# A feed-forward layer taken tile by tile instead of in pairs, with its keys as rows, and a second buffer of probabilities

## What is computed

```python
x = x + xattn(layernorm(x), ctx)     # 8 heads of 128; ctx has 2 x 77 = 154 rows of 384
x = x + ffn(layernorm(x))

# xattn: sim = q k^T * 128**-0.5, (sim - mean) * 1.5 + mean, softmax over 154 keys, times v, heads joined, Wout, + bout
# ffn, over the rows t of a batch:
x_prev = concat([zeros, x[:, :-1, :]])
xr = mu_r * x + (1 - mu_r) * x_prev
xk = mu_k * x + (1 - mu_k) * x_prev
out = sigmoid(xr @ W_r) * (square(relu(xk @ W_k)) @ W_v)
```

## Time and profile before

| | before |
|---|---|
| three timed runs, median (lowest to highest) | 744.74 us (743.87 to 744.83) |
| the profiled execution, its own time | 744.54 us |
| its span, first to last instruction | 742.7 us |
| TensorE busy | 736.4 us, 99% of the span |
| VectorE, ScalarE, GpSimd busy | 516.0, 426.8, 123.7 us |
| moved by DMA | 106.52 MB, mean 143 GB/s |

### The profile page before, as it was taken

One profiled execution on the slowest core, in us unless ns is written; L12 is line 12 of the kernel. 1 busy time (PEld: TensorE's weight loads), 2 busy tenths in 40 slices (PEclk: granted clock), 3 DMA queues, 4 the chain that ended last, 5 costly groups with the idle time before them and its releaser, 6 DMA issues.

```text
span 742.7 us, 13556 instructions
## 1 busy us (share of the span) xinstructions
PE 736.4 (99%) x3948; PEld 643.0 (87%) x3948; DVE 516.0 (69%) x1085; ACT 426.8 (57%) x1204; POOL 123.7 (17%) x279
## 2 busy tenths in 40 slices
PE   9999999999999999999999999999999999999998
PEld 8957888888988888898888889888888988888887
DVE  3678987777667766666776766677666667766662
ACT  3568865575746556564655656465665646565332
POOL 1111111202121120212112021211202121120211
PEclk9999999999999999999999999999999999999999
...
GB/s 330 252 152 172 202 136 115 148 147 177 140 146 147 117 164 87 176 142 167 129 109 159 93 175 144 163 126 115 167 84 175 143 167 128 109 156 93 112 28 43
DMA packets 87239, 106.52 MB, mean 143 GB/s; under 512 B 9999, under 2 KB 64169, under 8 KB 87211
## 3 DMA queue, kind: packets, MB, share of 16 engines
...
HBM read 58.70 MB, written 47.45 MB: 143 GB/s over the span
## 4 chain that ended last, share of the span: by engine, by line
PE 90%; SPq 5%; DVE 1%; DMA 1%; ACT 1%; issue 1%; POOL 0%; POOLq 0%; DVEq 0%
PE ffn L494 12%; PE ffn L496 12%; PE ffn L495 12%; PE scores L495 9%; PE scores L496 9%; PE scores L494 9%; PE attended L496 9%; PE attended L495 9%; PE attended L494 9%; SPq L353 3%; SPq L336 1%; PE attended L544 1%; PE attended L543 1%; DMA x_rows<-normed 1%; SPq L333 1%
## 5 line engine op out<-in xcount | busy, mean ns | idle before, releaser
L494 PE MATMUL scores<-A_hi,xT_hi 128*128 128x462 f32 x372 | 129.9, 349 | 0.8 <-DVE B_lo L973 0.8
L495 PE MATMUL scores<-A_lo,xT_hi 128*128 128x462 f32 x372 | 130.4, 351 | 0.0
L496 PE MATMUL scores<-A_hi,xT_lo 128*128 128x462 f32 x372 | 130.0, 349 | 0.0
L775 ACT ACTIVATE probs<-scores,neg_max 128x154 f32<-128x154 f32 x248 | 93.2, 387 | 46.7 <-DVE neg_max L1033 46.6
L496 PE MATMUL attended<-B_hi,pT_lo 128*128 128x512 f32 x288 | 112.5, 391 | 0.0
L495 PE MATMUL attended<-B_lo,pT_hi 128*128 128x512 f32 x288 | 112.4, 390 | 0.0
L494 PE MATMUL attended<-B_hi,pT_hi 128*128 128x512 f32 x288 | 112.1, 389 | 0.0
L1033 DVE TENSOR_REDUCE neg_max<-scores 128x3 f32<-128x462 f32 (+1 forms) x93 | 53.3, 581 | 80.9 <-PE scores L496 80.9
L1334 POOL TENSOR_SCALAR var<-stats 128x1 f32<-128x1 f32 x64 | 13.2, 206 | 462.4 <-DVE stats L979 461.3
L494 PEld LDWEIGHTS scores<-A_hi,xT_hi 128*128 128x128 f32 x372 | 70.2, 189 | 8.0 <-issue 1.7
L495 PEld LDWEIGHTS scores<-A_lo,xT_hi 128*128 128x128 f32 x372 | 70.1, 188 | 5.6
...
## 6 DMA issues: line engine op xcount, KB each, us to landing
...
probs_handed<-prob_rows SPq DMA_DIRECT2D x128, 176.0 KB, 3.4
...
```

Source lines behind the costliest of these rows:

```text
L494: te.matmul(psum, left[0], right[0], start=first, stop=False)
L495: te.matmul(psum, left[0], right[1], start=False, stop=False)
L496: return te.matmul(psum, left[1], right[0], start=False, stop=last)
L775: last = nc.scalar.activation(probs[:, q, cols], score_banks(t)[b][:, (h - h0) * J:(h - h0 + 1) * J], ACT.Exp, bias=neg_max[:, h:h + 1], a ...
```

## The change

The feed-forward part goes tile by tile, one step behind attention. In step t TensorE makes scores(t + 2), attend(t), `key_rows`(t - 1), `gate_rows`(t - 1) and `value_rows`(t - 2). `key_rows` takes the tile as stationary operand and the weights as moving one: 12 matmuls of 512 columns. Its result has rows on the partitions, so the squares now take the road through DRAM as well: `store_squares`, `hand_squares` (five DMAs more for a tile on SyncE's queue), `squares_turn` on VectorE; for the last tile TensorE turns them (`turn_last_squares`, 4 transposes). `handed2` and `act_handed` are landing buffers of their own, there are two buffers `probs`, the halo is kept for every tile and not for every pair, `add_x` stands ahead of `x_turn`, probabilities are handed back one step later, and in the ramp the first exponentials of tile 1 stand ahead of the first `values_hi`. W_v's raw rows land elsewhere, after a wait for `wq_turned`. The ramp on each engine and the last steps are rewritten for the new order. The core of the diff:

```diff
         handed = sb("handed", [P, D])
+        handed2 = sb("handed2", [P, D])
...
-        probs = sb("probs", [P, 4, WIDE])
-        probs_high = probs[:].bitcast(F32R)
+        probs = [sb(f"probs{i}", [P, 4, WIDE]) for i in range(2)]
+        probs_high = [p[:].bitcast(F32R) for p in probs]
...
-            mixed[w] = sb(f"x{w}", [P, DC, 2 * P])
-            mixed_lo[w] = sb(f"x{w}_lo", [P, DC, 2 * P], F32R, at=at_mixed)
-            mixed_hi[w] = sb(f"x{w}_hi", [P, DC, 2 * P], F32R)
-        at_act = cursor[0]
-        act = sb("act", [P, DC, 2 * P])
-        act_lo = sb("act_lo", [P, DC, 2 * P], F32R, at=at_act)
-        act_hi = sb("act_hi", [P, DC, 2 * P], F32R)
+            mixed[w] = sb(f"x{w}", [P, DC, P])
+            mixed_lo[w] = sb(f"x{w}_lo", [P, DC, P], F32R, at=at_mixed)
+            mixed_hi[w] = sb(f"x{w}_hi", [P, DC, P], F32R)
+        act = sb("act", [P, D])
+        act_handed = sb("act_handed", [P, D])
+        at_actT = cursor[0]
+        actT = sb("actT", [P, DC, P])
+        act_lo = sb("act_lo", [P, DC, P], F32R, at=at_actT)
+        act_hi = sb("act_hi", [P, DC, P], F32R)
         at_gate = cursor[0]
...
+            def store_squares(t):
+                sp.wait_ge(square_ready, t + 1)
+                sp.dma_start(act_dram[bass.ds(t * P, P), :], act[:]).then_inc(act_stored, 16)
+
+            def hand_squares(t):
+                sp.wait_ge(act_stored, 16 * (t + 1))
+                if begun(t - 1):
+                    sp.wait_ge(act_turned, t)
+                hand(act_handed, act_dram, t, act_landed)
...
+            def key_rows(t):
+
+                if begun(t - 1):
+                    te.wait_ge(relu_ready, t)
+                else:
+                    te.wait_ge(W_ready, DC)
+                te.wait_ge(mixed_split["k"], t + 1)
+                ffn_rows(T[1], (mixed_hi["k"], mixed_lo["k"]), WT["k"]).then_inc(k_done, 1)
+
...
-            def key_columns(q):
-
-                te.wait_ge(mixed_split["k"], 2 * q + 2)
-                for j in range(2):
-                    if begun(q - 1):
-                        te.wait_ge(gated, 2 * q + j - 1)
-                    for m in (2 * j, 2 * j + 1):
-                        for c in range(DC):
-                            cols = tuple(w[:, c, m * P:(m + 1) * P] for w in WT["k"])
-                            last = three_passes(T[1 + j][:, (m % 2) * 2 * P:(m % 2 + 1) * 2 * P], cols,
-                                                (mixed_hi["k"][:, c, :], mixed_lo["k"][:, c, :]),
-                                                c == 0, c == DC - 1)
-                    last.then_inc(k_done, 1)
-
...
+            def turn_last_squares():
+
+                te.wait_ge(square_ready, TILES)
+                for c in range(DC):
+                    last = te.transpose(S[1][:, c * P:(c + 1) * P], normed[:, c * P:(c + 1) * P], identity[:])
+                last.then_inc(act_turned, 1)
+
...
             def step(g, s):
-                t, q, half = place(g, s)
+                t = place(g, s)
                 if is_tile(t + 2):
                     scores(t + 2)
                 if is_tile(t):
                     attend(t)
-                if is_pair(q) and half == 0:
-                    gate_rows(q, 0)
-                    key_columns(q)
-                if is_pair(q) and half == 1:
-                    gate_rows(q, 1)
-                    value_rows(q, 0)
-                    if is_last(t):
-                        turn_last_x2()
-                    if is_pair(q + 1):
-                        value_rows(q, 1)
-                    else:
-                        last_value_rows()
+                if is_last(t):
+                    value_rows(t - 3)
+                key_rows(t - 1)
+                gate_rows(t - 1, turn_last_x2 if is_last(t) else None)
+                if is_last(t - 1):
+                    turn_last_squares()
+                if not is_last(t + 1):
+                    value_rows(t - 2)
+                if is_last(t - 1):
+                    last_value_rows()
...
+            scores(4)
+            attend(2)
+            key_rows(0)
+            gate_rows(0)
+            scores(5)
+            key_rows(1)
+            gate_rows(1)
+            attend(3)
+            value_rows(0)
+            key_rows(2)
+            gate_rows(2)
+            value_rows(1)
             turns(te, step)
...
+            def squares(t):
+                act_e.wait_ge(k_done, t + 1)
+                if is_last(t):
+                    act_e.wait_ge(xn_stored, 16 * (TILES - 2))
+                if begun(t - 1):
+                    act_e.wait_ge(act_stored, 16 * t)
+                nc.scalar.activation(act[:], T[1][:], ACT.Relu).then_inc(relu_ready, 1)
+                act_e.wait_ge(relu_ready, t + 1)
+                to, rows = (in_quarters(normed), by_quarter(act)) if is_last(t) else (act[:], act[:])
+                nc.scalar.activation(to, rows, ACT.Square).then_inc(square_ready, 1)
+
...
             def step(g, s):
-                t, q, half = place(g, s)
-                if is_pair(q) and half == 1:
-                    squares(q, 1)
-                    squares_hi(q)
+                t = place(g, s)
                 if comes_in_steps(t + 3):
                     x_norm(t + 3, (s + 3) % 4)
                 if is_tile(t + 2):
-                    for b in range(3):
-                        exponentials(t + 2, b)
-                    normalise_early(t + 2)
-                if is_tile(t - 1):
-                    mixed_high("k", t - 1, 1 - half)
-                    mixed_high("r", t - 1, 1 - half)
+                    exponentials(t + 2, s % 2, 0)
+                mixed_high("k", t - 1)
+                if is_tile(t + 2):
+                    exponentials(t + 2, s % 2, 1)
+                if not is_last(t) and not is_last(t - 1):
+                    squares_hi(t - 2)
+                mixed_high("r", t - 1)
+                if is_tile(t + 2):
+                    exponentials(t + 2, s % 2, 2)
+                    normalise_early(t + 2, s % 2)
+                    pack_hi(t + 2, s % 2)
                 if is_tile(t + 3):
                     x_hi(t + 3)
-                if is_tile(t + 2):
-                    pack_hi(t + 2)
-                if is_pair(q):
-                    open_gate(q, half, t)
                 if is_tile(t):
                     x2_norm(t, s)
+                if is_last(t) or is_last(t - 1):
+                    squares_hi(t - 2)
+                squares(t - 1)
                 if is_tile(t + 1):
                     for i in range(3):
                         probs_hi(t + 1, i)
-                if is_pair(q) and half == 0:
-                    squares(q, 0)
+                open_gate(t - 1, (s + 1) % 2)
+                if is_last(t - 1):
+                    squares_hi(t - 1)
 
             nc.scalar.dma_start(ctx1[:], ctx_rows[P:J, :]).then_inc(ctx_loaded, 16)
...
+                exponentials(0, 0, b)
+            normalise_early(0, 0)
+            pack_hi(0, 0)
             x_norm(3, 3)
-            for b in range(2):
-                values_hi(2 * b)
-                values_hi(2 * b + 1)
-                exponentials(1, b)
+            exponentials(1, 1, 0)
+            for b in range(1, 3):
...
-            normalise_early(4)
+                exponentials(4, 0, b)
+            normalise_early(4, 0)
             x_hi(5)
-            mixed_high("r", 1, 1)
-            open_gate(0, 0, 2)
-            pack_hi(4)
+            pack_hi(4, 0)
+            squares(0)
             x2_norm(2, 2)
+            mixed_high("k", 1)
             for i in range(3):
                 probs_hi(3, i)
-            squares(0, 0)
-            turns(act_e, step, from_second=True)
+            open_gate(0, 0)
+            x_norm(6, 2)
+            mixed_high("r", 1)
+            for b in range(2):
+                exponentials(5, 1, b)
+            squares_hi(0)
+            exponentials(5, 1, 2)
+            normalise_early(5, 1)
+            squares(1)
+            mixed_high("k", 2)
+            pack_hi(5, 1)
+            x_hi(6)
+            open_gate(1, 1)
+            mixed_high("r", 2)
+            squares_hi(1)
...
             for w in "kr":
-                mix(w, 0, 0, 0)
+                mix(w, 0)
             for b in range(3):
                 maxima(4, b)
             for w in "kr":
-                mixed_low(w, 0, 0)
-            x2_turn(1, 1, 0)
-            mix_change(1, 1, 0)
-            mix("k", 1, 1, 0)
+                mixed_low(w, 0)
             inverse_early(4)
-            mixed_low("k", 1, 1)
+            x_turn(5)
+            normalise_late(4, 0)
+            x_lo(5)
+            x2_turn(1)
+            pack_lo(4, 0)
+            mix_change(1)
             add_x(2, 0, 2)
-            normalise_late(4)
-            x_turn(5)
-            mix("r", 1, 1, 0)
-            x_lo(5)
-            mixed_low("r", 1, 1)
-            pack_lo(4)
             probs_turn(3)
+            mix("k", 1)
```

(48 more changed lines are left out.)

448 lines of the change are left out of this document (232 added, 216 removed).

## The result

The changed kernel took **742.38 us** (median of 9 executions, 741.68 to 743.74), the kernel before, run beside it, 744.18 (743.03 to 745.71): ratio 0.9976, 95% interval 0.9967 to 0.9984, so 1.8 us less (below, the interval stands in brackets behind each ratio). Run once more later, it gave 742.25 and 0.9975 [0.9963, 0.9987]. The forecast of 744.8 was 2.4 too high; it said "no change" and there is a small gain.

The account below looks back on a forecast made before the run. TensorE, busy 99% of the span, was taken as the bound. -5.1 - 0.1 + 1.5 + 1.1 + 2.0 + 0.8 + 0.4 - 0.5 = +0.1 us on 744.74 gave 744.8; range 741.2 to 747.8 for 8 in 10.

Parts of the forecast that it names:

- 1.1 us ahead of value_rows(1): Ramp: TensorE waits 1.1 us for open_values(0) before tile 1's value rows; bounds 0 and 2.5.
- 0.8 us ahead of turn_last_squares: Last steps: TensorE waits 0.8 us for squares(31), behind tile 30's squares through DRAM; bounds 0 and 2.
- the start, -0.1: Start: only 0.1 us saved, as tile 0's probabilities come back at 60.6 us regardless; bounds 0 and 1.9.
- Wait 1.5 us in front of gate_rows(1): Ramp: TensorE waits 1.5 us, xr's high part standing behind x_norm(6) on ScalarE; bounds 0.5 and 2.5.
- Keys, -5.1: TensorE's key rows: 384 matmuls of 512 columns replace 768 of 256, saving 5.1 us; bounds 4.6 to 5.6.
- The loop adds nothing: Tiles 4 to 28: no added wait, step 21.47 us; least reserve 2 us at the squares, 4 more behind.
- Rival B: Loop: the squares' way through DRAM holds each step, landing 6 us later than walked; slower, 749.8 us; 12%.
- Wait 2.0 us ahead of attend(31): Last steps: TensorE waits 2.0 us for probs_hi(31), squares(29) standing in front on ScalarE; bounds 1.0 and 2.5.
- Old wait -0.5: Last steps: the earlier 0.5 us wait ahead of the turn of the last tile's second x goes.
- transposes +0.4: TensorE's four new transposes for the last tile's squares add 0.4 us.
- Rival A: Other engines run ahead of the walk, three of four waits vanish; faster, 739.4 to 742.5 us; 22%.
- four gaps that sum to under 3 us: Sign of being wrong: the four TensorE waits in ramp and last steps sum to under 3 or over 8 us.

Follow-up runs that it names:

- a0: The changed kernel, unedited, run and profiled a second time in a later call: 742.25 us, ratio 0.9975 to the kernel before.
- k1: Changed kernel with each tile's key rows made as two halves of 256 columns, 768 matmuls instead of 384: 747.72 us.
- s1: Changed kernel with SyncE returning a tile's squares one step later, behind the return of the next probabilities: 872.84 us.
- t1: Changed kernel with ScalarE, in tile 30's step, making the squares of tile 29 behind the three copies probs_hi(31): 742.95 us.
- t2: Changed kernel with eight matmuls whose result nobody reads put on TensorE ahead of attend(31): 742.76 us.
- b1: Changed kernel with ScalarE's start as in the kernel before: tile 1's exponentials behind the value blocks, waiting for tile 0's stored probabilities: 742.53 us.
- b2: Changed kernel with eight small loads of the mixing vectors moved later on SyncE's queue, behind returns of tile 0's probabilities and tile 3's x: 742.12 us.
- t3: Changed kernel with ScalarE making xr_hi of tile 1 ahead of the normalisation of tile 6: 742.44 us.
- u1: Changed kernel with xr_hi of tile 1 ahead of x_norm(6) on ScalarE and open_values(0) ahead of squares_turn(1) on VectorE: 741.09 us.
- u3: Changed kernel with xr_hi(1) and open_values(0) made earlier, mixing-vector loads moved later, and eight unread matmuls ahead of attend(31): 739.79 us.

## Why the prediction was wrong, step by step

The steps that failed are two waits of the sum: 1.1 us ahead of value_rows(1), measured 0 to 0.17, and 0.8 us ahead of turn_last_squares, measured 0. Two smaller sizes erred to the same side (gate_rows(1), 1.5 for 0.9, and the start, -0.1 for -0.5), and a term was missing, 0.5 ahead of key_rows(31). Against the undisturbed profile, a0 (span 740.6, 2.1 under 742.7):

- **Keys, -5.1.** Right: step, tile and k1 agree.
- **The loop adds nothing.** Right, with the reserve as walked (2.8 + 4.1 where 2 + 4 was said). Rival B is out, though s1 shows that its real danger is the ring through SyncE's queue, which the prediction did not look at.
- **The start, -0.1.** Half right. Measured -0.5 (85.51 to 85.02). From the first value block scores(4) came 1.84 earlier, but in a0 the blocks began 1.35 later (47.20, 45.85 before), and there TensorE did not wait for the probabilities at all: their turn was no fixed point at 60.6 "whatever the others do", it lay between 57.7 and 60.7. The queue held the start, as forecast, in the first profile. scores(2) was said near 56.9 and stood at 57.94 and 58.31. That the term came out near -0.1 is in part luck; whether the change itself moves the blocks was not tried.
- **"Wait 1.5 us in front of gate_rows(1)".** Cause right to the instruction, size 0.9 to 1.0. In the first profile xr's low part was ready at 114.27 instead of 115.1: 0.3 because the whole ramp ran ahead (xr's low part of tile 0 ended at 96.46, walked 96.8), 0.5 over the chain of twelve terms. TensorE came at 113.42 instead of 113.6.
- **"Wait 1.1 us" ahead of value_rows(1).** This is the step that failed most. Measured 0 and 0.17 (0.3 to 0.5 in t1, t2, b1, b2). The walk had value_rows(1) ready at 133.7 and TensorE there at 132.7; in the first profile the opened values were ready at 131.83 and TensorE was there at 131.99. VectorE turned the squares at 126.82 instead of 128.6. Of these 1.8 us, 0.9 lie ahead of the store: squares(1) ended at 120.87 instead of 121.8, nearly all of it inherited from the wait before (0.8). The other 0.9 are the way through DRAM: SyncE issued the store at 120.90 and the first return at 122.94. From store to return are 2.0 where the walk had 2.8 "with probabilities in flight"; from there to the turn 3.9 of 4, though in this profile the row names TensorE's value rows as what released the turn (in a0, at 126.80, the landing). SyncE's queue and VectorE in the first profile:

```profile
120.90 0.36 SPq L408 DMA_DIRECT2D square_rows<-act  x1
122.94 1.74 SPq L370 DMA_DIRECT2D act_handed<-square_rows  x4
```
```profile
126.82 0.71 DVE L1047 STREAM_TRANSPOSE actT<-act_handed 128x512 f32<-128x512 f32 x1 [0.46 <-PE ffn L516]
...
131.18 0.65 DVE L1159 SCALAR_TENSOR_TENSOR gate<-gate,ffn 128x512 f32<-128x512 f32 x1
```

  Behind the turn the walk (5.1) was right. The wait itself was real: t3, whose store went out earlier and took longer to come back (118.94 to 122.34, 3.4), uncovers it with 1.56.
- **Wait 2.0 us ahead of attend(31).** Right in size (1.93 to 1.97) and cause (t1: 0.83 against 0.8). That removing it gains nothing was not seen, and what it does to the clock neither.
- **"Wait 0.8 us" ahead of turn_last_squares.** Failed: none. squares(31) ended 37.9 after attend(30)'s start (walked 38.1), but TensorE came at 38.06 instead of 37.35. Of these 0.7 the wait of 0.46 ahead of key_rows(31), which the walk did not have, is the larger part, and it covers this one: a wait earlier on TensorE's path that is overlooked makes every later one look longer than it is.
- **Old wait -0.5, transposes +0.4.** Right: the wait is gone, and the four new transposes took 0.36 us of TensorE in the first profile (732.96 - 732.60).

What the undisturbed profile shows adds up: -5.1 - 0.5 + 0.9 + 0.2 + 1.9 + 0.5 + 0.4 - 0.5 = -2.2, against -2.1. 3.5 us of new waits stand where 5.4 were forecast. Rival A (739.4 to 742.5) wanted three of four to vanish; two all but did and a third shrank by 0.5, so the outcome lies between it and the forecast. The prediction's own sign for being wrong, four gaps that sum to under 3 us, came true by a hair: 2.95 in the first profile, 2.97 in a0. That 742.4 is not 742.2 or less is in part the clock, 0.24 on average.

So of the gain of 5.1 us, 3.5 went into new waits in the ramp and the last steps and 0.4 into transposes; the old wait and the start gave 1.0 back. u1 shows that 1.3 us were still to be had by two orders in the ramp; u3 reached 2.5, in part for a reason that stays open.
